# Cosine attention of an eight-stage kernel, rewritten with transposed heads in pairs and without barriers

## The reference

```python
q = (x @ w_q).reshape(b, s, h, -1).transpose(0, 2, 1, 3)
kv = x @ w_kv
k, v = jnp.split(kv, 2, axis=-1)
...
q = _l2norm(q) * jnp.exp(scale)
k = _l2norm(k)
sim = jnp.einsum('bhid,bhjd->bhij', q, k)
attn = jax.nn.softmax(sim, axis=-1)
out = jnp.einsum('bhij,bhjd->bhid', attn, v)
out = out.transpose(0, 2, 1, 3).reshape(b, s, h * out.shape[-1])
return out @ w_out + b_out
...
x = x + _L1_attn_ref(_layernorm(x, axis=-1), ...)
```

## Time and profile before

| | us |
|---|---|
| median of 3 runs | 7300.73 (7299.51 to 7301.55) |
| the profiled execution | 7293.42 |
| its span | 7291.5 |
| the stage, between its barriers | 1029 |

### The profile page before, as it was taken

One profiled execution on the slowest core, in us unless ns is written; L12 is line 12 of the kernel. 1 busy time (PEld: TensorE's weight loads), 2 busy tenths in 40 slices (PEclk: granted clock), 3 DMA queues, 4 the chain that ended last, 5 costly groups with the idle time before them and its releaser, 6 DMA issues. The chain is left out here.

```text
span 7291.5 us, 130088 instructions
## 1 busy us (share of the span) xinstructions
PE 6447.3 (88%) x51713; PEld 3888.3 (53%) x51713; DVE 4398.8 (60%) x7622; ACT 3585.7 (49%) x5896; POOL 2013.4 (28%) x1333
## 2 busy tenths in 40 slices
PE   7999978999986666689965899999999999999998
PEld 4666656676773222256643455555555555555554
DVE  3444433222304888833344788888888888888885
ACT  3434424454522334334433466665666666666664
POOL 0000000000001334300000455555555555555553
PEclk9999978898956778789976899999999999999999
DMA  1000000000000000000000111111111111111111
GB/s 49 1 1 1 1 0 1 1 1 1 1 24 5 0 0 0 0 1 0 0 1 20 30 33 42 39 33 40 38 33 42 39 33 42 39 33 45 38 38 27
DMA packets 146538, 141.31 MB, mean 19 GB/s; under 512 B 19781, under 2 KB 137062, under 8 KB 145766
## 3 DMA queue, kind: packets, MB, share of 16 engines
q1 hardware_dynamic: 145990, 133.59, 7.7%
HBM read 30.77 MB, written 2.10 MB: 5 GB/s over the span
## 5 line engine op out<-in xcount | busy, mean ns | idle before, releaser
L2191 POOL TENSOR_TENSOR local_ssum<-local_sq 128x512 f32<-128x512 f32 x384 | 692.5, 1803 | 2296.8 <-ACT local_sq L1979 2296.2
L2199 POOL TENSOR_TENSOR local_rot<-local_rot,local_inv_all 128x512 f32<-128x512 f32 x768 | 961.6, 1284 | 90.7 <-DMA local_inv_all<-local_inv 89.9
L1800 PE MATMUL banks<-local_y,local_Wqkv 128*128 128x512 f32 x1536 | 823.7, 618 | 63.8 <-ACT local_sq L1979 61.0
L2001 ACT ACTIVATE local_probs<-local_probs,local_npeak 128x1152 f32<-128x1152 f32 x384 | 482.7, 1257 | 355.2 <-DVE local_probs L2105 355.2
L2105 DVE TENSOR_TENSOR local_probs<-banks,band 128x576 f32<-128x576 f32 x768 | 546.3, 753 | 183.4 <-PE banks L1835 178.1
L2085 DVE TENSOR_TENSOR local_rot<-banks,local_rotary_scaled 128x512 f32<-128x512 f32 x768 | 526.0, 685 | 192.8 <-PE banks L1800 187.1
L823 POOL PARTITION_ALL_REDUCE int_allmax<-int_rowmax x1 | 0.4, 378 | 2187.0 <-issue 2187.0
L1979 ACT ACTIVATE local_sq<-banks 128x512 f32<-128x512 f32 x768 | 459.6, 598 | 244.2 <-DVE local_sin L2086 237.8
L1835 PEld LDWEIGHTS banks<-local_rot 32*128 32x128 f32 x12288 | 415.1, 185 | 224.8 <-issue 202.8
L2092 DVE TENSOR_TENSOR local_rot<-local_rot,local_sin 128x1024 f32<-128x1024 f32 x384 | 501.8, 1307 | 40.4 <-DVE local_sin L2086 0.5
L986 PE MATMUL banks<-mamba_seen,ident 128*128 128x512 f32 x512 | 325.6, 769 | 223.3 <-POOL mamba_seen L1060 223.2
(11 more groups left out here) (401 smaller groups left out, 11981.1 us busy)
## 6 DMA issues: line engine op xcount, KB each, us to landing
local_inv_all<-local_inv SPq DMA_DIRECT2D x768, 128.0 KB, 2.7
local_Wqkv<-in_L_ffn_Wqkv_quads SPq DMA_DIRECT2D x36, 256.0 KB, 3.0
local_Wo<-in_L_ffn_Wo_quads SPq DMA_DIRECT2D x6, 512.0 KB, 3.5
experts_w_W<-in_L_ffn_W SPq DMA_DIRECT2D x1, 2048.0 KB
out<-x SPq DMA_DIRECT2D x8, 256.0 KB, 2.3
local_W<-in_L_ffn_W SPq DMA_DIRECT2D x12, 170.5 KB, 2.3
cosine_w_Wqkv<-in_L_attn_w_kv SPq DMA_DIRECT2D x1, 1024.0 KB
mamba_drive<-in_pick SPq DMA_DIRECT2D x1, 768.0 KB, 5.2
```

The lines of the kernel that those rows point to most:

```text
L1800: pe.matmul(seqs(banks[:, QK_BANK, :]), Wqkv[:, at:at + P], y_group(g), start=True, stop=True).then_inc(qk_projected, 1)
L2001: act.activation(a, a, ACT.Exp, bias=npeak[:, layer:layer + 1], scale=SCALE).then_inc(exped, 1)
L2191: pool.tensor_tensor(ssum[:, n % 2, m, :], sq[:, 0, :], sq[:, 1, :], ALU.add).then_inc(square_summed, 1)
L2199: pool.tensor_tensor(a, a, twice(inv_all[:, n % 2, m, of_seq(s)]), ALU.mult).then_inc(united, 1)
```

## The change

q and k are now projected transposed: `project` has 128 columns of the weights (one pair of heads) as weights and 512 tokens as moving operand, so two heads lie on the two halves of the partitions and no transposes of q, k or y remain. VectorE copies q and k out; ScalarE squares them; `norm` sums the squares with four matmuls onto four column quarters of the array, `heads_of_pair` being the weights; VectorE clamps, ScalarE makes the inverse, four DMAs spread it over the 64 partitions of each head (`send_inverse`), and `unite` multiplies. `score` alternates between the heads of the pair, that is between the row halves of the array. `values` alternates between column halves and keeps queries on the moving side. The sums of the exponentials are four more matmuls per pair and sequence (two heads, two key tiles), ones times the exponentials, which leave the sum on all 64 partitions of a head; ScalarE inverts it by Ln and Exp over 128 x 512, and VectorE multiplies.

One block does all 64 pairs (n = 8 x group + pair); step i projects pair i, makes norms of i - 1, scores of i - 2, values of i - 3 and normalizes i - 4. All three projections of a step go through one bank, A_BANK. A v projection per step serves a tile and half of the heads of the group. The output is made per tile, in four of eight steps, and added per tile. Everything is straight code; the only barrier left is at the stage's end.

```diff
-        def step(heads_of, make_of, parity):
...
-                    def turn_qk(k):
...
-                    def turn_y(j):
...
+                def project(n, m):
+                    g = group_of(n)
+                    if m == 0:
...
+                        if n:
+                            pe.wait_ge(copied, 2 * n)
+                    else:
+                        pe.wait_ge(v_copied, n + 1)
+                    c = m * INNER + pair_of(n) * P
+                    pe.matmul(banks[:, A_BANK, :], w["Wqkv"][:, c:c + P], xnT[:, g % 2, :], start=True, stop=True).then_inc(qk_projected, 1)
+
+                def project_v(n):
+                    pe.wait_ge(copied, 2 * n + 1)
...
+                def norm(n):
+                    pe.wait_ge(squared, 2 * n + 2)
+                    take_x(clamped, n + 1)
+                    for c in range(4):
+                        last = pe.matmul(banks[32 * c:32 * c + 32, X_BANK, 0:SEQ], consts["heads_of_pair"], sq[:, c // 2, of_seq(c % 2)],
+                                         start=True, stop=True)
+                    last.then_inc(norm_summed, 1)
+
+                def score(n, s):
+                    pe.wait_ge(unit, 2 * n + 2)
+                    if n:
+                        pe.wait_ge(exped, 4 * (n - 1) + 2 * s + 2)
+                    q, k = (qk[:, n % 3, m, :] for m in range(2))
+                    for tile in range(ST):
+                        at = s * SEQ + tile * P
+                        for r in range(2):
+                            rows_r = slice(r * HD, (r + 1) * HD)
+                            last = pe.matmul(banks[:, S_BANK + 2 * s + r, tile * SEQ:(tile + 1) * SEQ], k[rows_r, at:at + P],
+                                             q[rows_r, of_seq(s)], start=True, stop=True)
+                    last.then_inc(scored, 1)
+
+                def values(n, s):
+                    g, j = group_of(n), pair_of(n)
+                    pe.wait_ge(exped, 4 * n + 2 * s + 2)
+                    pe.wait_ge(v_copied, PAIRS * g + j // GT * GT + 2 * s + 2)
+                    if s == 0 and n:
+                        pe.wait_ge(normalized, n)
+                    for tile in range(ST):
+                        for r in range(2):
+                            rows_r, c = slice(r * HD, (r + 1) * HD), (2 * j + r) * HD
+                            pe.matmul(banks[rows_r, O_BANK, of_seq(s)], v[:, g % 2, s * ST + tile, c:c + HD], probs[:, n % 2, s, r, tile, :],
+                                      start=(tile == 0), stop=(tile == ST - 1))
+                    for tile in range(ST):
+                        for r in range(2):
+                            rows_r = slice(r * HD, (r + 1) * HD)
+                            last = pe.matmul(banks[rows_r, DEN_BANK, of_seq(s)], consts["ones"][:, 0:HD], probs[:, n % 2, s, r, tile, :],
+                                             start=(tile == 0), stop=(tile == ST - 1))
+                    last.then_inc(valued, 1)
...
+                for i in range(FIRST, LAST + 1):
+                    if within(i) is not None:
+                        project(i, 0)
+                    if (n := within(i - 1)) is not None:
+                        norm(n)
+                    if within(i) is not None:
+                        project_v(i)
+                    if (n := within(i - 2)) is not None:
+                        score(n, 0)
+                    if within(i) is not None:
+                        project(i, 1)
+                    if (n := within(i - 2)) is not None:
+                        score(n, 1)
+                    if (n := within(i - 3)) is not None:
+                        values(n, 0)
+                        values(n, 1)
+                    if (g := group_at(i, 2 - PAIRS)) is not None:
+                        turn_x(g)
+                    if (tile := tile_at(i)) is not None:
+                        project_out(tile)
...
+                def invert_den(n):
+                    act.wait_ge(valued, 2 * n + 2)
+                    if n:
+                        act.wait_ge(normalized, n)
+                    act.activation(rden[:], banks[:, DEN_BANK, :], ACT.Ln).then_inc(den_logged, 1)
+                    act.wait_ge(den_logged, n + 1)
+                    act.activation(rden[:], rden[:], ACT.Exp, scale=-1.0).then_inc(rden_ready, 1)
```

386 lines of the change are left out of this document (193 added, 193 removed).

## The result

The changed kernel takes 7047.23 us, the median of 4 runs (7041.65 to 7059.99); the kernel before took 7301.14 beside it. The ratio is 0.966 (95% interval 0.964 to 0.967). The profiled execution took 7041.65 us, with a span of 7039.9.

The account below looks back on a forecast made before the run. TensorE was taken as the bound: work 684, waits 65, start and end 20 and clock 8 give a 777 us stage, 252 less than 1029. That made 7048 us for the kernel, range 7020 to 7075 with 0.72.

Parts of the forecast that it names:

- work of the stage: TensorE's work in the changed stage: 64 steps of 9.42, 32 output tiles and 8 turns of x, 684 us against 813.
- (a): Value projection waits for VectorE's query copy, queued behind an earlier pair's normalization: 1.2 to 1.3 us a step.
- (b): In steps with an output tile (four of eight) only the query's own copy counts: about 0.3 us of wait.
- (c): Key projection waits for ScalarE's copy of v, behind a square, Ln and Exp: 0.1 us.
- (d): The turned x and the new group's normalization add about 1.5 us once a group.
- start, end and clock: Thin first steps about 17 us, 3 more at the end, and 8 us for the clock.
- Rival 2: Array halves do not overlap in scores and values: 5.2 us more a step, 7365 us, slower; chance 3%.
- upper bound: Kernel at 7100 us, from a shape change at twice its row (40 us) or the clock falling for a few stretches.
- Rival 4: The waits of (a) are smaller than reckoned: kernel at 7010 to 7025 us; chance 7%.
- rival 1: TensorE's short gaps lower the granted clock; at 1.2 GHz throughout 7590 us; strong form 3%, weak 8%.
- weak form: Of rival 1: a clock dip per group (0.91), costing 45 to 60 us, 7100 us; chance 8%.
- rival 3: Inverses land late, breaking 0.7 us of slack: 1.2 us a step, 32 to 64 times, 7090 to 7120 us; chance 7%.

Follow-up runs that it names:

- experiment 2: Changed kernel with the key projection moved behind the second sequence's scores, so the two score groups are neighbours: 7036.2 us.
- experiment 3: Changed kernel with the ones matmuls of the second key tile left out, so the sums hold half of the exponentials: 6994.8 us.
- Experiment 6: Changed kernel with the scores of both heads taken from rows 0 to 63, the other rows idle for scores: 7191.7 us.
- experiment 4: Changed kernel with both key tiles of one head before the other's in scores, values and sums, four instructions at a time: 7057.0 us.
- experiment 5: Changed kernel with all values and ones matmuls of a pair written for one head, then the other, sixteen instructions each: 7225.5 us.
- experiment 1: Changed kernel with VectorE's normalization moved behind the clamp, so the query copy stands ahead of it: 7024.0 us.
- experiment 7: Changed kernel with VectorE's normalization and the next group's LayerNorm both moved behind the clamp: 7006.3 us.
- experiment 10: Changed kernel with the four transfers of a pair's inverse lengths sent twice, first to a spare buffer: 7100.0 us.
- experiment 8: Changed kernel with both heads' scores from rows 0 to 63, and VectorE's normalization and LayerNorm behind the clamp: 7110.3 us.
- experiment 11: Changed kernel with GpSimd adding the two key tiles of the exponentials, so TensorE multiplies by ones once: 7011.5 us.
- experiment 12: Changed kernel with normalization and LayerNorm behind the clamp, key projection behind the second scores, and GpSimd adding the key tiles: 6955.1 us.

## Why the prediction was right, point by point

The median was forecast at 7048 and measured at 7047.2. That closeness is partly chance: the terms were off by up to 15 us, both ways. In us of the stage, worked out from the steps of the trace:

| term | forecast | measured |
|---|---|---|
| TensorE's work in a step | 9.42 | 9.54 (9.75 less the 0.21) |
| work of the stage | 684 | 692 |
| wait for the query copy, steps without an output tile (a) | 1.2 to 1.3 | 1.06 |
| the same with one (b) | 0.3 | 0.21 |
| wait of the key projection (c) | 0.1 | none (1.06 start to start) |
| LayerNorm, once a group (d) | 1.5, eight times | 1.35, six times |
| waits in all | 65 | about 50 |
| start, end and clock | 28 | 28 (what is left of 770) |
| stage | 777 | 770 |
| steps without / with an output tile | 10.8 / 12.2 | 10.60 (9.75 right behind a step with a tile) / 12.15 |

The wait stands at a step's start, so its size goes by the step before. A group in the middle has it eight times: 0.21 four times, 1.06 twice, 0.57 behind the turn of x and 2.41 behind the LayerNorm, 5.9 us together where the forecast had 8.1.

- **The bound.** That TensorE's row sets the pace, and that what the change takes from it comes back as time, held in full: work went down by 121 (813 to 692; forecast 129), waits came to 50 (65), and what is left of the 259, clock and barriers together, is 188 (forecast 146 + 42). No run splits the 188; that it matches the forecast says no more than that the stage did. Experiments 2 and 3 are the cleanest proof: 0.20 and 0.87 us less on TensorE were 0.20 and 0.87 us less a step.
- **The halves.** Half price for scores, values and sums, read off a single place of the trace before, was right (1.06 and 3.61). Experiment 6 has the other side: 1.92 and 109 us for the scores. Rival 2 is out. What I took for granted and did not write is that the order of the heads matters little: true up to four instructions of one head in a row (experiment 4), but at sixteen it costs 164 us (experiment 5).
- **The change of shape.** The prediction called it 0.09 a change. Experiment 2 took one change of seven out of the step and got 0.20. Both come from the same rows: a group next to one change takes 0.95 instead of 0.86, one between two takes 1.05, so a change costs about 0.10 in the group ahead of it and 0.10 in the group behind. My group prices (1.05) held both halves, which is why the sum was right; the single figure, and the 40 us reckoned from it for the upper bound, counted only one. The Trainium skill (TensorEngine Tiling (Array Packing), Key Properties) says that such a change drains the TensorE; the 0.20 is in line with a drain dearer than I granted.
- **The sums of squares.** The step's term for them was too small: 0.64 for their own work and, with the 0.21 of wait, 0.85 against 0.57. The earlier trace rows showed 0.57 for instructions in the middle of others; here they are followed by a wait, so the end of the last one is seen. That is most of the 0.12 by which the work was short.
- **The waits.** The mechanism of (a), VectorE's normalization ahead of the query copy, was right and confirmed by experiment 1; its size was 0.2 too large. In that chain Ln (0.60), Exp (0.63), normalization and copy (0.69 and 0.68) came out as priced. From the end of the sums' slot to the value projection the lines of the step at 1204.35 have 2.75 us where I had 2.9: Ln starts 0.11 behind the slot's end and not 0.20, and the copy's record starts 0.08 before the normalization's ends. And queries and norm sums cover 1.69 of it, not 1.62. Rival 4 (7010 to 7025) was this effect in a stronger form and did not happen.
- **The clock, rival 1.** Neither form occurred: 0.98 in the stage, one fall of 3.4 us besides the 17 us at the start and short ones in the last steps. But the run with half of the rows idle shows the weak form as forecast, a fall once per group, for 40 us, and what it takes: the 2.4 us that TensorE waits once a group. The falls in the full steps of the changed kernel and of experiments 1 to 5 (3.4 us, twice 6.8) stand in the step of this wait too, but not behind every one: behind 13 of 30 waits of 2.4 us and three of six of 1.8 us (experiment 1). They are gone in experiment 7. The Trainium skill (TensorE: Matmul & The Clock Gate, A second HAM failure mode) blames such oscillation on short idle times between groups of matmuls; these runs agree, with the addition that 1.06 us idle in each of five steps in a row (the first group) did no harm here, and the single 2.4 us often did.
- **The inverses, rival 3.** Not late in the changed kernel. The 0.7 us of slack was of the right kind and somewhat small. In the changed kernel's trace the way from the Exp's end to the product takes 4.5 to 5.6 us, where the earlier trace rows had 5.8. The slack can be read there too: behind the slowest ones, as here, the products run from 1214.11 to 1215.40, and the normalization behind them could not start before the inverted sums at 1216.35, so 0.95 us are left; other steps without an output tile have up to 2.0. That fits experiment 10, whose 2.5 us more are over it.
- **The rest of the kernel.** "Untouched" was right to within its scatter (6261 to 6290 in the profiled executions), which is larger than several terms of the sum. It took back the 7 us that the stage gained over the forecast: that is the luck in 7048 against 7047.2.

## What to carry to other kernels

When one engine is busy nearly all the time, write its row of work start to start and price each piece from a stage that already does the same: here that gave a stage of 770 us to 1%. Then look at the order of the engine that hands its input back: a copy that the bound engine waits for belongs ahead of everything else in its queue, and the rarest, longest such wait is worth removing first, since the clock can add to its length (15 us for the LayerNorm's place, of which the six waits are 10, and 39 us of clock where rows are idle). Work can be moved to an idle engine by the look of its row, but check which of its neighbours read the same memory: GpSimd's addition was free by its own time (1.41 us on average) and still added a quarter to a half to the mean time of VectorE's products.

## What the runs showed of the hardware that I had not expected

- **TensorE starts matmuls out of program order.** With sixteen instructions for one half of the columns and then sixteen for the other, the first of the second sixteen starts beside the thirteenth of the first, four places ahead of its turn, and only four overlap (experiment 5, 1405.79, and so in all 64 pairs). With four and four, all overlap (experiment 4, halves of columns and of rows).
- **What stood before the falls of the clock.** An idle time of 2.41 us was followed by a fall of 13.7 us in six groups of six when scores used half of the rows. When they used all rows, a fall of 3.4 or 6.8 us followed in some groups: one of six in the changed kernel, five of six in experiment 2, which differs from it by the place of one projection. Half-idle rows without the wait had none in the full steps (experiment 8; one of 3.4 us came in the thin last ones). Idle times of 3.5 us with all rows in use gave falls of 3.4 to 6.8 us. What decides between a fall and none behind the same wait stays open.
- **GpSimd and VectorE take turns where both read two operands from SBUF.** The pair of 128 x 512 products took 2.37 us instead of 1.29 where GpSimd's addition came between, and the addition 1.81 instead of 1.27 (experiment 11). Copies out of PSUM did not mind: in experiment 12, 64 of the 128 ran beside an addition for over nine tenths of their time and took 0.69 us on average, as the others did. VectorE's product with a PSUM operand never met an addition, so these runs say nothing of it.
